# Attention units of 4 head groups x 32 queries, with V laid out by 4 heads x 32 keys

## The reference

```python
q, k, v = layernorm(x) @ Wq.T, ctx @ Wk.T, ctx @ Wv.T        # split into 16 heads of 8
scores = einsum('bhqd,bhkd->bhqk', q, k) * 8 ** -0.5
scores = where(q_index >= k_index, scores, -1e9)              # causal: 64 queries, 64 keys
x = x + (softmax(scores) @ v) @ Wo.T
z = layernorm(x)
rw = softmax(z.mean(over the batch's rows) @ Wr + br)         # one choice of experts for a batch
x = x + layernorm(sum of the top 2 experts' gelu(z W1 + b1) W2 + b2, + z) * gamma + beta
```

## Time and profile before

| | us |
|---|---|
| median of three runs | 685.32 |
| the profiled execution | 685.26 |
| its span in the trace | 683.5 |
| TensorE busy | 619.5 |
| ScalarE busy | 487.8 |
| VectorE busy | 457.5 |
| GpSimd busy | 358.2 |

### The profile page before, as it was taken

How to read it: one execution, slowest core, us unless ns; L and a number is a source line. 1 busy time by engine, 2 the same in 40 slices (tenths; PEclk the granted TensorE clock), 3 DMA queues, 4 the chain that set the end, 5 groups by cost and what they waited for, 6 DMA issues and landing times.

```text
span 683.5 us, 20582 instructions
## 1 busy us (share of the span) xinstructions
PE 619.5 (91%) x5067; PEld 497.2 (73%) x5067; DVE 457.5 (67%) x1439; ACT 487.8 (71%) x1101; POOL 358.2 (52%) x538
## 2 busy tenths in 40 slices
PE   4899999999999999999949617999999999999882
PEld 3677777777777777777737415999999999998872
DVE  3999998989898989898939661333333333333696
ACT  3788888888888888888838513665666666665585
POOL 5778888888888888888846630000000000000585
PEclk9999999999999999999989756999999999999997
DMA  3010221012101211021271102322232322321033
GB/s 109 25 32 10 63 58 57 15 54 61 54 29 40 61 54 43 26 61 38 64 227 33 37 27 73 96 85 85 80 87 80 87 81 84 85 82 42 31 109 108
DMA packets 85339, 44.02 MB, mean 64 GB/s; under 512 B 7737, under 2 KB 84289, under 8 KB 85313
## 3 DMA queue, kind: packets, MB, share of 16 engines
q1 hardware_dynamic: 85312, 43.70, 22.0%
HBM read 30.83 MB, written 12.85 MB: 64 GB/s over the span
## 4 chain that ended last, share of the span: by engine, by line
PE 83%; DVE 7%; issue 3%; SPq 2%; ACT 2%; DMA 1%; POOL 0%; DVEq 0%; POOLq 0%; ACTq 0%
PE banks L475 17%; PE bank L344 16%; PE bank L356 8%; PE banks L369 6%; PE bank L382 5%; PE bank L341 5%; PE bank L465 5%; PE bank L467 5%; PE bank L466 5%; PE bank L330 3%; PE bank L322 2%; PE bank L318 2%; PE bank L392 2%; DVE ln_stats L904 2%; PE bank L317 2%
## 5 line engine op out<-in xcount | busy, mean ns | idle before, releaser
L649 ACT ACTIVATE q_by_row_group<-bank,b_all 128x256 f32<-128x256 f32 x268 | 126.9, 474 | 95.5 <-PE bank L467 95.5
L893 DVE SCALAR_TENSOR_TENSOR yT<-banks,slot_weight,yT x268 | 73.0, 284 | 145.6 <-PE banks L475 139.7
L1042 POOL TENSOR_TENSOR probs<-probs,row_sum_recip 128x512 f32<-128x512 f32 x128 | 133.5, 1043 | 65.8 <-DVE row_sum_recip L780 63.8
L475 PE MATMUL banks<-q_by_row_group,w_all 128*128 128x256 f32 x536 | 159.6, 380 | 0.0
L344 PE MATMUL bank<-k_by_head,q_by_row_group 128*128 128x256 f32 x512 | 132.9, 383 | 0.0
L465 PE MATMUL bank<-gathered,w_hi 128*128 (+1 forms) x268 | 126.5, 472 | 4.5 <-DMA gathered<-z_split 4.5
L1088 POOL TENSOR_TENSOR w_lo<-w_all,w_hi 128x512 fp32r<-128x512 f32 x8 | 10.2, 1274 | 190.7 <-ACT w_hi L629 190.7
L344 PEld LDWEIGHTS bank<-k_by_head,q_by_row_group 128*128 128x128 f32 x512 | 99.3, 194 | 14.3
L764 DVE TENSOR_REDUCE row_max<-bank 128x8 f32<-128x512 f32 x128 | 88.0, 687 | 29.7 <-PE bank L344 29.6
L591 ACT ACTIVATE probsT<-bank 128x512 f32<-128x512 f32 x128 | 76.4, 597 | 28.0 <-PE bank L356 26.3
L767 DVE TENSOR_REDUCE row_sum<-probs 128x8 f32<-128x512 f32 x128 | 86.8, 678 | 10.7 <-ACT probs L582 10.2
(11 more groups left out here) (148 smaller groups left out, 1013.8 us busy)
## 6 DMA issues: line engine op xcount, KB each, us to landing
gathered<-z_split SPq DMA_DIRECT2D x272, 64.0 KB, 1.8
z_split<-z_hi_lo SPq DMA_DIRECT2D x32, 256.0 KB, 2.6
x_res<-in_x SPq DMA_DIRECT2D x16, 256.0 KB, 2.9
ctxT_pair<-in_ctxT SPq DMA_DIRECT2D x32, 128.0 KB, 2.1
w_all<-in_w SPq DMA_DIRECT2D x16, 256.0 KB, 4.5
out<-k_by_head SPq DMA_DIRECT2D x16, 256.0 KB, 2.3
z_split<-yT SPq DMA_DIRECT2D x2, 128.0 KB, 2.5
wq<-in_wq SPq DMA_DIRECT2D x1, 64.0 KB, 2.5
```

What stands on the lines that cost most here:

```text
L475: nc.tensor.matmul(ps, W2F[:, e, c, :], G[:, c, :], start=(c == 0), stop=(c == FC - 1)).then_inc(p_c, 1)
L649: nc.scalar.activation(G[:, c, :], bank[c][:, 0:BT], ACT.Gelu, bias=B1A[:, e, c:c + 1]).then_inc(a_g, 1)
L1042: nc.gpsimd.tensor_tensor(pp, pp, RC[:, k % 2, :].unsqueeze(2).to_broadcast([128, 8, S]), ALU.mult).then_inc(g_norm, 1)
```

## The change

A pair becomes three units of 512 scores per partition (`NU = 3 * NP`) instead of four. A partition is now one of four row groups of 32 queries. Unit `LOW` holds the first 32 queries of all four batches and only their first 32 keys. `HIGH_A` and `HIGH_B` hold the last 32 queries of two batches each, with all 64 keys. The mask comes behind the scores, over 512 columns in LOW and over the second 256 columns in a HIGH unit.

Each `steps` is rewritten for three units. Instructions of VectorE and GpSimd on HIGH units have views with one dimension more (`rows_of`, `spread`, `as_lies`). `attend` works by two batches (a tile): 16 matmuls of 64 or 32 columns, each in a group of 32 array columns, against V laid out by 4 heads x 32 keys. `prep_v` becomes 32 matmuls of 32 columns and ScalarE's copy of V four pieces of 32 partitions. `project` is one matmul against the unchanged `WO` and writes into the tile's own `A_ps` bank; `WOZ` and its set-up go. `prep_v` moves from the last step of the pair before to the second step of its own pair, and its copy to the last step. `turn_z` moves to the last step, and waits for this pair's V copy; `keep_z` and what follows it move about two thirds of a pair later.

The core of the diff (`steps` of VectorE and GpSimd, set-up and the host's layouts of the weights are left out; removed lines of any length stand in the functions above):

```diff
+NU = 3 * NP
+LOW, HIGH_A, HIGH_B = range(3)
+HALF = S // 2
...
+        def rows_of(t, kind):
+            if kind == LOW:
+                return t.rearrange("p (n k) -> p n k", k=HALF)
+            return t.rearrange("p (h n k) -> p n h k", h=2, k=HALF)
+        def spread(t, kind):
+            if kind == LOW:
+                return t[:, 0:16].unsqueeze(2).to_broadcast([128, 16, HALF])
+            return t[:, 0:8].unsqueeze(1).unsqueeze(3).to_broadcast([128, 2, 8, HALF])
+        def as_lies(t, kind):
+            if kind == LOW:
+                return t.rearrange("p (n k) -> p n k", k=HALF)
+            return t.rearrange("p (h n k) -> p h n k", h=2, k=HALF)
...
+            def prep_v(P, par):
+                ge(pe, a_zt, P - 3)
+                for n in range(8):
+                    for j in range(4):
+                        mm = nc.tensor.matmul(J1[32 * j:32 * j + 32, 32 * n:32 * n + 32],
+                                              CT[:, par, HALF * n:HALF * n + HALF], WV[:, j, :], start=True, stop=True)
                 mm.then_inc(p_v, 1)
...
+            def scores(P, U, kind, par, ps):
+                if kind == LOW:
                     ge(pe, a_q, P + 1)
                     ge(pe, g_km, P + 1)
                 ge(pe, v_sub, U - 1)
...
+                if kind == LOW:
+                    for b in range(4):
+                        nc.tensor.matmul(ps[:, 128 * b:128 * b + 128],
+                                         QR[:, par, b, 0, :, :].rearrange("p r q -> p (r q)"), KM[:, par, b, :, 0:HALF],
+                                         start=(b == 0), stop=False, skip_group_check=True)
+                    masked, keys = ps[:, :], cmask[:, :, :].rearrange("p a k -> p (a k)")
+                else:
+                    for n in range(2):
+                        b = 2 * (kind - HIGH_A) + n
+                        nc.tensor.matmul(ps[:, :].rearrange("p (h b c) -> p h b c", h=2, b=2)[:, :, n, :],
+                                         QR[:, par, b, 1, :, :].rearrange("p r q -> p (r q)"),
+                                         KM[:, par, b, :, :].rearrange("p j (h k) -> p h j k", h=2),
+                                         start=(n == 0), stop=False, skip_group_check=True)
+                    masked, keys = ps[:, 256:512], cmask[:, 0:8, :].rearrange("p a k -> p (a k)")
+                nc.tensor.matmul(masked, identb[:, :], keys,
+                                 start=False, stop=True, skip_group_check=True).then_inc(p_s, 1)
+            def turn(U, slot, half):
                 ge(pe, g_norm, U + 1)
                 ge(pe, a_pt, U - 1)
...
+                for n in range(4):
+                    mm = nc.tensor.transpose(T_ps[half][:, 128 * n:128 * n + 128],
+                                             PP[:, slot, 128 * n:128 * n + 128], ident[:, :])
                 mm.then_inc(p_t, 1)
...
+            def attend(T, t, P, par):
+                ge(pe, a_pt, 3 * P + 2 + t)
+                ge(pe, a_v, P + 1)
+                ge(pe, v_x2, T - 1)
+                for n in range(2):
+                    b = 2 * t + n
+                    for kh in range(2):
+                        for r in range(4):
+                            rows = slice(32 * r, 32 * r + 32)
+                            if kh == 0:
+                                cols, probs = slice(S * n, S * n + S), PT[:, par, b, 0:2, rows]
+                            else:
+                                cols, probs = slice(S * n + HALF, S * n + S), PT[:, par, b, 2, rows]
+                            mm = nc.tensor.matmul(A_ps[t][rows, cols],
+                                                  VM[:, par, 2 * b + kh, r, :, :].rearrange("p j d -> p (j d)"),
+                                                  probs, start=(kh == 0), stop=(kh == 1), skip_group_check=True)
                 mm.then_inc(p_pv, 1)
...
+            def project(T, t):
                 ge(pe, a_at, T + 1)
...
+                nc.tensor.matmul(A_ps[t][:, 256:256 + D], AT[:, t, :], WO[:, :], start=True, stop=True).then_inc(p_w, 1)
+            def turn_z(P, v_before):
+                ge(pe, a_z, P + 1)
                 ge(pe, a_v, v_before)
...
                 for k in range(2):
                     mm = nc.tensor.transpose(J1[:, 128 * k:128 * k + 128], ZZ[:, k, :], ident[:, :])
                 mm.then_inc(p_zt, 1)
...
+                for u in range(6):
+                    P, U, s, h = 2 * i + u // 3, 6 * i + u, u % 3, u // 3
+                    now, ahead = not static or P < NP, not static or P + 1 < NP
+                    if now:
+                        scores(P, U, s, h, S_ps[u % 2])
+                    if s == 0 and ahead:
                         pe.wait_ge(d_ct[(h + 1) % 2], 16 * i + 16 * (h + 1))
                         prep_xk(P + 1, (h + 1) % 2)
+                    if not static or 0 <= P - 1 < NP:
+                        turn(U - 3, (u - 3) % 6, (u - 3) % 2)
+                    if s == 1 and ahead:
+                        prep_q(P + 1)
                     if s == 0 and (not static or 0 <= P - 2 < NP):
...
+                        attend(4 * i + (2 * h - 3), 1, P - 2, h)
+                        project(4 * i + (2 * h - 4), 0)
+                    if s == 1 and (not static or 0 <= P - 2 < NP):
+                        project(4 * i + (2 * h - 3), 1)
+                    if s == 1 and now:
+                        prep_v(P, h)
                     if s == 2 and (not static or 0 <= P - 1 < NP):
...
+                        attend(4 * i + (2 * h - 2), 0, P - 1, 1 - h)
+                    if s == 2 and (not static or 0 <= P - 3 < NP):
+                        turn_z(P - 3, P + 1 if not static else min(P + 1, NP))
...
+                ge(act, p_pv, 2 * P - 2)
+                for j in range(4):
+                    rows = slice(32 * j, 32 * j + 32)
+                    nc.scalar.activation(VM[rows, par, :, :, j, :],
+                                         J1[rows, 0:256].rearrange("p (n r d) -> p n r d", r=4, d=HD),
+                                         ACT.Copy).then_inc(a_v if j == 3 else a_vh, 1)
...
+            def take_probs(P, U, kind, half, par):
+                act.wait_ge(p_t, U + 1)
+                if kind == LOW:
+                    ge(act, p_pv, 2 * P - 2)
+                    turned, to = T_ps[half][:, :].rearrange("p (b t) -> p b t", t=128), PT[:, par, :, 0, :]
+                else:
+                    b = 2 * (kind - HIGH_A)
+                    turned = T_ps[half][:, :].rearrange("p (k b t) -> p k b t", k=2, b=2)
+                    to = PT[:, par, b:b + 2, 1:3, :].rearrange("p b k t -> p k b t")
+                nc.scalar.activation(to, turned, ACT.Copy).then_inc(a_pt, 1)
+            def take_attn(T, t):
+                act.wait_ge(p_pv, T + 1)
+                ge(act, p_w, T - 1)
+                nc.scalar.activation(AT[:, t, :], A_ps[t][:, 0:128], ACT.Copy).then_inc(a_at, 1)
             def steps(i):
                 static = isinstance(i, int)
...
+                for u in range(6):
+                    P, U, s, h = 2 * i + u // 3, 6 * i + u, u % 3, u // 3
+                    now, ahead = not static or P < NP, not static or P + 1 < NP
+                    if s < 2 and (not static or 0 <= P - 2 < NP):
+                        take_attn(4 * i + (2 * h - 4 + s), s)
+                    if not static or 0 <= U - 1 < NU:
+                        act.wait_ge(v_sub, U)
+                        ge(act, p_t, U - 6)
+                        nc.scalar.activation(PP[:, (u - 1) % 6, :], SS[:, (u - 1) % 2, :], ACT.Exp,
+                                             scale=SCALE).then_inc(a_exp, 1)
+                    if s == 0 and ahead:
+                        prep_xk(P + 1)
+                    if s == 0 and (not static or 0 <= P - 4 < NP):
+                        keep_z(P - 4, h, None if static else i - 1)
+                    if s == 2 and ahead:
+                        prep_q(P + 1, (h + 1) % 2)
+                    if not static or 0 <= P - 1 < NP:
+                        take_probs(P - 1, U - 3, s, (u - 3) % 2, 1 - h)
+                    if s == 2 and now:
                         prep_v(P, h)
...
+                    if s == 2 and (not static or P + 2 < NP):
                         norm1(P + 2)
...
+                    if s == 1 and (not static or 0 <= P - 3 < NP):
                         norm2(P - 3)
...
```

More of the change, by code:

```diff
@@ L340, in scores @@
                 ge(pe, v_sub, U - 1)
[L341 to L347, removed]
@@ L397, in steps @@
                 static = isinstance(i, int)
-                for u in range(8):
-                    P, U, s, h = 2 * i + u // 4, 8 * i + u, u % 4, u // 4
-                    more = not static or P + 1 < NP
-                    if not static or U < NB:
-                        scores(i, u)
-                    if not static or 0 <= U - 3 < NB:
-                        turn(i, u - 3)
-                    if not static or 0 <= U - 4 < NB:
-                        attend(i, u - 4)
```

(27 more changed lines are left out.)

240 lines of the change are left out of this document (78 added, 162 removed).

## The result

The changed kernel takes 708.13 us (median of 4 runs, 706.36 to 708.79), the kernel before, run beside it, 684.49 (4 runs): a ratio of 1.034, 95% interval 1.0313 to 1.0368. It is 23.6 us slower, where 4 us faster was forecast, and outside the predicted range.

What follows compares the result with a forecast made beforehand. TensorE's stream was taken to bound the attention loop, and a ring through the V copy to bound it after the change. 685.3 - 9 (ring) - 6 (ends) + 11 (clock) = 681 us, range 666 to 695.

Steps and rivals of the forecast that it cites:

- the ring: Attention loop: V copy, z transposes, next pair's scores and copies wait on each other, 10.9 us a pair against 11.25.
- the gap of 2.65 us ahead of the z transposes: TensorE finishes each pair's work about 2.65 us before ScalarE's V copy lets the z transposes start.
- TensorE's 8.25 us a pair: Sum of TensorE's work per pair in the attention loop, 8.25 us against 11.25 before.
- the attend group's 0.60: One TensorE group of 32 small attend passes, estimated at 0.5 to 0.7 us, taken as 0.60.
- V's 0.75: TensorE's 64 V passes per pair, estimated at 0.7 to 1.1 us, taken as 0.75.
- ScalarE's three waits of 0.9, 0.37 and 0.41: Per pair, ScalarE waits 0.9 us for the key matmul, 0.37 for HIGH_A's transposes, 0.41 for HIGH_A's exponential input.
- The price of a half-clock stretch, 1.7 us: A fall to half clock between the V copy and HIGH_A's turn costs the pair 1.7 us.
- The rival by which small passes cost issue time: Attend and V passes cost 0.039 us each, ring 11.65, no gap: 690 us, or 695 at 0.045; chance 0.12.
- I take one pair in four: Assumed share of the loop's 26 pairs in which TensorE's clock falls to half, adding 11 us.
- the ends: First three pairs about 2 us earlier, z-transfer wait about 1 less, drain about 3 less: together -6, within -10 and 0.
- bounds of 0 and 44 us: Limits of the clock's cost in the loop: no fall, 0; a fall in every one of 26 pairs, 44 us.
- the clock decides: Rival: frequent falls at the gap ahead of the z transposes; nine cancel the gain, every second pair gives 692; chance 0.18.

Runs made afterwards that it cites:

- e1: Changed kernel plus ten dummy matmuls of 128 columns behind each pair's first attend group, in TensorE's gap: 681.48 us, ratio 0.997 to the kernel before.
- e2: Changed kernel plus four dummy matmuls of 128 columns behind each pair's first attend group: 695.49 us, ratio 1.0172 to the kernel before.
- e3: Changed kernel with the z transposes moved behind the next pair's key pass: 688.88 us, ratio 1.0076 to the kernel before.
- e10: Changed kernel, z transposes behind next key pass, key spreads in second step, normalisation before V copy, shift before subtraction, statistics one step earlier, no dummies: 663.51 us.
- e8: Changed kernel with z transposes behind the next pair's key pass, plus eight dummy matmuls in TensorE's gap: 672.01 us, ratio 0.982 to the kernel before.
- e7: Changed kernel with the four reorders of e6, plus six dummy matmuls in TensorE's gap: 684.00 us, ratio 0.9995 to the kernel before.
- e6: Changed kernel, z transposes behind next key pass, key spreads in second step, normalisation before V copy, shift before subtraction: 686.12 us, ratio 1.0028 to the kernel before.

## Why the prediction was wrong

**Right.** TensorE stops being the bound, and the ring decides: the gap of 2.65 us ahead of the z transposes measured 2.59 to 2.67, TensorE's 8.25 us a pair 8.35, the attend group's 0.60 is 0.48, V's 0.75 is 0.69, ScalarE's three waits of 0.9, 0.37 and 0.41 are 0.69, 0.43 and 0.31. The ring of 10.9 is 11.03 where the loop does not turn. The price of a half-clock stretch, 1.7 us, is 1.72 by e1 and 1.63 by e2. GpSimd releases nothing of TensorE's in the pair above; its key spread became the last wait only when e3 opened the ring. Its normalisation takes 1.05 us in the new view, for 1.04 before.

The rival by which small passes cost issue time is out: 32 passes in 0.48 us are 15 ns apiece. By the Trainium skill (TensorEngine Tiling (Array Packing), section Instruction Overhead) the attend group was estimated at 1.0 us; across column groups this trace does not agree, and the measurement decides.

**Wrong: the step "I take one pair in four".** In the forecast's own terms:

| term | predicted | measured |
|---|---|---|
| ring at full clock, 26 pairs | -9 | +0.9 = 26 x (11.284 - 11.25) |
| half-clock stretches | +11, some 6.5 of them | +25.8, 15 of them |
| the ends | -6 | -3.7 |

The first failure is the count, +15 us. I had bounds of 0 and 44 us, and took a value near the lower one because three quarters of a pair are dense work and a last stage with many short gaps had kept its clock. That row speaks for short gaps, and so does e10; the new gap was one long one, the only row with a longer one had the clock at half behind it, and the fall at 384.8 had come without any long gap. The rival "the clock decides" had the right place and price, and 0.18 of the chances. With the measured count it gives 670 + 15 x 1.7 = 695.5; the rest of the way to 708 is the ring and, for 2 us, the ends. Its nine falls until the gain is gone rested on a ring of 10.9 as well: by e1's 681.5, two would have done.

The second is the ring, +10 us, 11.28 for 10.9. From one start of the z transposes to the next, the changed kernel's pairs at full clock take 11.03 and, where the loop turns, 11.57 to 11.62; in e1 they take 11.01 and 11.56 to 11.61 in turn. So 0.13 a pair is the ring itself, and the loop's turn adds some 0.55 in every second pair, 0.27 a pair, which was no item of mine. TensorE's wait ahead of the LOW scores at 155.81 is 0.31 of it; what makes that wait is not shown. Without any half-clock stretch the change is worth 0.3%, the 681.5 of e1: the 3 us of TensorE's work that it saves per pair are nearly all taken back by the ring.

The ends are off by 2 us: the first pairs take 1.4 us more up to pair 4, where 2 less were forecast (one half-clock stretch, from 26.1, lies among them), and the rest gave 5 us for 4.

Whether the gap could also be closed by giving V and z a bank of their own was not tried. Nor is it shown why ten stretches came with gaps of 1.6 and of 2.5 us alike (e2, e3).

## What to carry to other kernels

When an edit makes the bounding engine idle, write down its longest single wait in each period and price the clock at that: here single waits of 1.5 to 2.7 us came with 9 to 15 half-clock stretches in 26 pairs, loops whose waits kept to 1.0 us had none (e10's one followed a wait of 1.75), and the stretches alone turned a gain of 2 us into a loss of 24. That is no assurance for other mixes: at the loop's end the kernel before fell to half clock with no wait over 1.1 us, TensorE busy for 2.9 of 4.5 us. Then look for the ring that holds the engine, and open it at every item that ends within some 0.5 us of the last one: one reorder moved the wait, five together (e10) turned the change into 3% less than before. Dummy work in the gap is a cheap way to find out on the chip what the clock costs: e1, e2 and e8 told it, e7 beside e6 did not.

## What the runs showed of the hardware

- TensorE's granted clock fell to 0.50 for 3.4 us at a time, in a kernel in which the engine is busy for three quarters of each pair at 1.00. Dummy matmuls of 2.50 us a pair (e1) took all 15 stretches away, 1.16 us (e2) left 10.
- In column groups, passes of 64 and 32 columns take 15 ns apiece and of 32 columns 11 (64 in 0.69), the change of shape included.
- In the changed kernel and in e1 TensorE waits some 0.3 us ahead of its first matmul at each turn of its loop; in the kernel before, where it was 99.9% busy, and in e8, where it waits there for the key spread, pairs show no such turn.
- Each of the 15 stretches of the changed kernel begins 0.6 to 1.8 us behind the end of a wait of TensorE of 2.6 to 2.7 us.
